# Attention scores in three terms, the low keys over 64 rows of the array

## The chip, the cores and the metric

The kernel runs on one core of one Trainium2 chip. The metric is the device time in microseconds. The engines are TensorE (PE, its weight loads PEld), VectorE (DVE), ScalarE (ACT), GpSimd (POOL) and the queue of SyncE (SP).

## The reference

Two layers over x of 2 x 1024 tokens of width 128. The part that the change touches is the attention of the first layer, 16 heads of width 64 over 1024 tokens of each of 2 batches:

```python
q = (x @ w_q).reshape(b, s, h, -1).transpose(0, 2, 1, 3)
k, v = jnp.split(x @ w_kv, 2, axis=-1)          # each to heads, as q
q = _l2norm(q) * jnp.exp(scale)
k = _l2norm(k)
sim = jnp.einsum('bhid,bhjd->bhij', q, k)
attn = jax.nn.softmax(sim, axis=-1)
out = jnp.einsum('bhij,bhjd->bhid', attn, v)
return out.transpose(0, 2, 1, 3).reshape(b, s, h * 64) @ w_out + b_out
```

After it come a residual and layer norm, a mixture of 8 experts (2 for each token), a norm, a state-space scan, a norm, a second mixture with a shared expert, and a norm. None of these is touched.

## The kernel before

The kernel holds numbers in two 16-bit parts, a high part (the number rounded to fp16, or cut to bf16 for the probabilities) and a low part (what is left), so that matmuls of fp16 come near to the precision of fp32.

The attention is cut into slots. A unit (h in the code, 16 of them) is two heads of one batch, and `bat` says which of its two heads. A slot is one head, 256 queries (QW) and 512 keys (KT = 4 key tiles of 128), so a head of a unit has 4 x 2 = 8 slots, a unit has SLOTS = 16, and there are 16 x 16 = 256 slots. The loop `heads` emits, on each engine, 32 slots (two units) for each i. In slot s:

- TensorE computes the scores (`scores`, L490) into the PSUM tile SC[s % 2], two banks of 512 columns, then the products of attention and values of the slot three before (`av`, L508; LAG = 3) into OP. In some slots it also transposes and multiplies the attention output of earlier units (L542, L550), projects tiles of the next unit (`proj`, L471 to L473) and transposes the next unit's queries and keys (`transposes`, L476, matmuls at L486). The slots of each of these are written out by hand in the tables GROUP_AT, TURN_AT, OUT_TURN_AT and OUT_AT.
- ScalarE takes the exponential of SC into Pr (L688), reads projections out of PSUM (L657, L658), makes the high part of the values (L665) and copies most of the transposes from the PSUM bank M1 into QK (L670).
- VectorE makes the low part Pl of the probabilities in 14 of 16 slots (L804), normalizes queries and keys (L777), casts their high parts into the stack `stk` (L786), copies the high keys a second time (L791) and reads OP (L823, L827).
- GpSimd makes Pl in the other two slots (L1033), inverse norms (L1040), low values (L1048) and the low parts of queries and keys (L1055).

The stack `stk` has, for each of 4 groups g of 4 token tiles, five cells of 64 columns (STK = 5 * DH): high queries, low queries, high keys, low keys, high keys again. `transposes` turns three pairs of neighbouring cells (128 columns each) into the three kinds of QK, each with 128 rows: kind 0 is high over low queries, kind 1 high over low keys, kind 2 low over high keys. A score is then two matmuls over 128 rows. Kind 1 times kind 0 gives high x high plus low x low, and kind 2 times kind 0 gives the two mixed terms:

```python
rhs = QK[:, b, 0, bat * S + q * QW:bat * S + q * QW + QW]
eng.matmul(out, QK[:, b, 1, key:key + P], rhs, start=True, stop=False)
mm = eng.matmul(out, QK[:, b, 2, key:key + P], rhs, start=False, stop=True)
```

The order around the change is kept by semaphores. Scores of slot n wait for the exponential of slot n - 2 (s_exps, L499), since SC has two buffers. The exponential waits for the scores and for a free Pr buffer (PB = 5, released by `av`). `av` waits for the low part of its slot (s_low_probs). The transposes wait for the high, copied and low parts of their group (s_qk_high, s_k_copied, s_qk_low). The first scores of a unit wait for the reads of all of its transposes.

Of the kernel before, what the change touches and what calls it, by code (L numbers as in the profile page):

```python
# [12 lines left out]
P = 128  # L13
B, S, D = 2, 1024, 128
T = B * S
NT = T // P
H, DH = 16, 64
# [8 lines left out]
def high(ap):  # L26

    return ap.bitcast(BF16)


def wait(eng, sem, count):

    if not isinstance(count, int) or count > 0:
        eng.wait_ge(sem, count)
# [12 lines left out]
QW = 256  # L47
KT = 4
# [6 lines left out]
TB = NT // B  # L55
# [28 lines left out]
def low_count(n, pool):  # L84

    mine = [k for k in range(SLOTS) if (k in POOL_LO) == pool]
    return n // SLOTS * len(mine) + sum(k <= n % SLOTS for k in mine)
# [44 lines left out]

CHUNK = 6
CHUNKS = 4


def chunk_tiles(c):

    return slice(CHUNK * c, min(CHUNK * c + CHUNK, TILES))


def sorted_rows(t):

    return t["w_or_rows"][:, 0:TILES * 2 * D].rearrange("p (j c) -> p j c", j=TILES)


def load_offsets(nc, t, ph, chunks=range(CHUNKS)):

    for c in chunks:
        _, values = nc.values_load_multi_w_load_instructions(  # L150
            t["at_w"][0:1, ph % 2, chunk_tiles(c)], engines=[mybir.EngineType.PE], min_val=0, max_val=(E - 1) * P,
            skip_runtime_bounds_check_because="the number of an expert was clamped to E - 1 before")
        for i, value in enumerate(values):
            t["weight_at"][ph, CHUNK * c + i] = value
# [96 lines left out]
def attention(nc, io, t):  # L251
# [3 lines left out]
    def sb(name, shape, dt):  # L255
        return es.enter_context(nc.sbuf_tensor(name, shape, dt))

    def ps(name, shape, dt):
        return es.enter_context(nc.psum_tensor(name, shape, dt))

    with es:
# [12 lines left out]
        nrm = sb("nrm", [P, 2, 4, 2, DH], F32)  # L274
        stk = sb("stk", [P, 4, 4, STK], F16)
        QK = sb("QK", [P, 2, 3, T], F16)
# [15 lines left out]
        SC = [ps(f"SC{i}", [P, KT, QW], F32) for i in range(2)]  # L292
# [29 lines left out]
        s_qk_high = sem("s_qk_high")  # L322
# [99 lines left out]
        def _(eng):  # L422
# [21 lines left out]
            rows = t["xs"][0].rearrange("(j p) c -> p j c", p=P)  # L444
            for c in range(CHUNKS):
                js = chunk_tiles(c)
                eng.dma_start(sorted_rows(t)[:, js, :], rows[:, js, :]).then_inc(s_rows_loaded, 16)
            eng.wait_ge(s_rows_loaded, 16 * CHUNKS)

        @block.tensor  # L450
        def _(eng):
# [24 lines left out]
            def transposes(h, j):  # L476
                g = j // 2

                wait(eng, s_qk_high, 4 * h + g + 1)
                wait(eng, s_k_copied, 4 * h + g + 1)  # L480
                wait(eng, s_qk_low, 4 * h + g + 1)
                m1 = M1[:, :].bitcast(F16)
                for kind in range(3):
                    at = (0, 2 * DH, 3 * DH)[kind]
                    for r in range(2):
                        mm = eng.transpose(m1[:, (2 * kind + r) * P:(2 * kind + r + 1) * P],  # L486
                                           stk[:, g, 2 * (j % 2) + r, at:at + P], ident16[:, :])
                mm.then_inc(s_turned, 1)

            def scores(i, s):  # L490
                n, h, b = 32 * i + s, 2 * i + s // SLOTS, s // SLOTS
                s %= SLOTS
                bat, q, kh = s // 8, s % 8 // 2, s % 2
                if s == 0:

                    wait(eng, s_turned_read_vector, 4)
                    wait(eng, s_turned_read_scalar, 8 * h + 4)

                wait(eng, s_exps, n - 1)  # L499
                for kt in range(KT):  # L500
                    key = bat * S + (kh * KT + kt) * P
                    rhs = QK[:, b, 0, bat * S + q * QW:bat * S + q * QW + QW]
                    out = SC[s % 2][:, kt, :]
                    eng.matmul(out, QK[:, b, 1, key:key + P], rhs, start=True, stop=False)  # L504
                    mm = eng.matmul(out, QK[:, b, 2, key:key + P], rhs, start=False, stop=True)  # L505
                mm.then_inc(s_scores, 1)

            def av(i, s):  # L508
                n, h, b = 32 * i + s, 2 * i + s // SLOTS, s // SLOTS
                s %= SLOTS  # L510
                bat, kh, u = s // 8, s % 2, s // 2

                pool = s in POOL_LO
                wait(eng, s_low_probs_pool if pool else s_low_probs, low_count(n, pool))
                if s == 0:

                    wait(eng, s_v_high, 4 * h + 4)
                    wait(eng, s_v_low, 4 * h + 4)
                if kh == 0:

                    wait(eng, s_outputs, 16 * i + 8 * b + u - 1)
                for kt in range(KT):
                    tile = bat * 8 + kh * KT + kt
                    for r in range(2):
                        hi = high(Pr[:, n % PB, kt, P * r:P * r + P])[:, 1::2]
                        lo = Pl[:, n % PB, kt, P * r:P * r + P]
                        at = (DH + 1) * r
                        first = kh == 0 and kt == 0 and r == 0
                        last = kh == 1 and kt == KT - 1 and r == 1
                        eng.matmul(OP[u % 2][:, at:at + 65], hi, V[:, b, tile, 0:65],  # L530
                                   start=first, stop=False, skip_group_check=True)
                        eng.matmul(OP[u % 2][:, at:at + 64], hi, V[:, b, tile, 65:129],  # L532
                                   start=False, stop=False, skip_group_check=True)
                        mm = eng.matmul(OP[u % 2][:, at:at + 65], lo, V[:, b, tile, 0:65],  # L534
                                        start=False, stop=last, skip_group_check=True)
                mm.then_inc(s_av_products, 1)
# [50 lines left out]
            def slot(i, s):  # L587
# [8 lines left out]
                if not ended(i):  # L596
                    scores(i, s)
                if s >= LAG and not ended(i):
                    av(i, s - LAG)
                elif s < LAG and started(i, 1):  # L600
                    av(i - 1, s + 2 * SLOTS - LAG)
# [34 lines left out]
            for j in range(PJ):  # L636
                m1_free(0, j, 0, 0)
                transposes(0, j)
# [120 lines left out]
        def _(eng):  # L759
# [20 lines left out]
            def high_parts(h, hb, g):  # L780
                G, b = 4 * h + g, g % 2
                wait(eng, s_normalized, G + 1)

                wait(eng, s_turned, 8 * (h - 1) + 2 * g + 2)
                out = stk[:, g, :, 0:4 * DH].rearrange("p t (k x) -> p t k x", k=2)[:, :, :, 0:DH]
                eng.tensor_copy(out, nrm[:, b, :, :, :]).then_inc(s_qk_high, 1)  # L786

            def copy_keys(h, hb, g):
                G, b = 4 * h + g, g % 2
# [237 lines left out]
        def _(eng):  # L1027
# [23 lines left out]
            def low_parts(h, hb, g):  # L1051
                G, b = 4 * h + g, g % 2
                wait(eng, s_qk_high, G + 1)
                both = stk[:, g, :, 0:4 * DH].rearrange("p t (k x) -> p t k x", k=2)
                eng.tensor_tensor(both[:, :, :, DH:2 * DH], nrm[:, b, :, :, :], both[:, :, :, 0:DH],  # L1055
                                  ALU.subtract).then_inc(s_qk_low, 1)

            def prepare(h, hb, s):
# [45 lines left out]
            for g in range(4):  # L1104
                if g < 3:
                    inverse_norms(0, 0, g + 1)
                low_values(0, 0, g)
                low_parts(0, 0, g)
# [82 lines left out]
def mixtures(nc, io, t, out):  # L1191
# [8 lines left out]
    with es:  # L1200
# [61 lines left out]
        s_gathered = [[sem(f"gathered{i}_{h}") for h in range(2)] for i in range(4)]  # L1262
        s_sorted_loaded = [sem(f"sorted_loaded{c}") for c in range(CHUNKS)]
        s_y_stored = [sem(f"y_stored{r}") for r in range(YR)]
# [18 lines left out]
        def _(eng):  # L1283
            def load(ph, c):
                J = TILES * ph
                js = chunk_tiles(c)

                eng.wait_ge(s_scattered[ph], 16 * 2 * TB)

                wait(eng, s_sorted_turned, J - TILES + js.stop)  # L1290
                rows = xs[ph % 2].rearrange("(j p) c -> p j c", p=P)
                eng.dma_start(xg[:, js, :], rows[:, js, :]).then_inc(s_sorted_loaded[c], 16)

            def store(ph, j):
                J = TILES * ph + j
                eng.wait_ge(s_down_read, J + 1)
                eng.dma_start(ys[ph % 2][P * j:P * j + P, :], yb[:, J % YR, :]).then_inc(s_y_stored[J % YR], 16)
# [22 lines left out]
            for j in range(TILES):  # L1320
                store(1, j)
            for c in range(CHUNKS):
                load(2, c)
            for j in range(TILES):
                store(2, j)
            for c in range(CHUNKS):
                load(3, c)
# [752 lines left out]
```

## Time and profile before

| | |
|---|---|
| time, median of 3 runs | 1051.43 us (1051.28 to 1055.02) |
| the profiled execution | 1044.7 us, its span 1042.9 us |
| mean granted TensorE clock | 0.944 of full |
| PE busy | 911.9 us, 87% |
| PEld busy | 856.1 us, 82% |
| ACT busy | 768.9 us, 74% |
| DVE busy | 732.2 us, 70% |
| POOL busy | 503.0 us, 48% |
| L504 and L505, scores | 1024 matmuls each, 273 ns each bar |
| L530, L532, L534, attention times values | 2048 matmuls each, 191 to 195 ns each bar |

A bar of a matmul is longer than the time until the next one starts, because matmuls are pipelined and their ends are modelled; the time that one costs TensorE is the distance between two starts. The span is divided in 40 slices of 26 us. The attention takes about the first 24 of them.

### The profile page before, as it was taken

The numbers are of one execution on the slowest core, as the hardware profiler recorded it, in microseconds if no ns is written. First come the engines' busy times: TensorE is split into PE (matmuls) and PEld (weight loads), VectorE is DVE, ScalarE is ACT, GpSimd is POOL, SyncE is SP. The second block draws the span as 40 slices with busy tenths as digits, with TensorE's granted clock in tenths as the row PEclk, the third lists the DMA queues.
The fourth block names the chain that finished last, engine by engine and source line by source line (L and its number), as shares of the span: only waits on it lengthen the run. The fifth ranks groups of instructions, "written<-read, shape, count | busy, mean of one in ns | idle before, by whom it ended". The sixth has DMA issues, their size and how long they took to land. (4 is left out here: it accounts for less than half of the span.)

```text
span 1042.9 us, 34710 instructions
## 1 busy us (share of the span) xinstructions
PE 911.9 (87%) x13676; PEld 856.1 (82%) x13676; DVE 732.2 (70%) x1432; ACT 768.9 (74%) x1275; POOL 503.0 (48%) x384
## 2 busy tenths in 40 slices
PE   4789999999999999999999997989969589899930
PEld 2678998998999989888889987989958479899830
DVE  6699989888988988888998974424549769400202
ACT  5689998998988999988889865445465366697831
POOL 5465655555554654644778800323327180052423
PEclk8799999999999999999999998999989689899965
DMA  8400000000000000000001020713111012023111
GB/s 256 130 2 3 23 3 23 2 3 22 3 3 22 3 3 23 3 3 23 9 8 37 13 63 7 231 55 91 45 29 31 1 36 64 16 72 98 57 57 43
DMA packets 43563, 42.13 MB, mean 40 GB/s; under 512 B 5648, under 2 KB 37392, under 8 KB 43408
## 3 DMA queue, kind: packets, MB, share of 16 engines
q1 hardware_dynamic: 39312, 31.51, 10.1%
q0 software_dynamic: 4096, 8.40, 2.6%
q8 instruction: 116, 1.90, 0.8%
q14 instruction: 39, 0.32, 0.1%
HBM read 25.60 MB, written 14.29 MB: 38 GB/s over the span
## 5 line engine op out<-in xcount | busy, mean ns | idle before, releaser
L688 ACT ACTIVATE Pr<-SC,nesc,esc 128x1024 f32<-128x1024 f32 x256 | 310.0, 1211 | 33.2 <-PE SC L505 22.9
L804 DVE TENSOR_TENSOR Pl<-Pr 128x1024 f16<-128x1024 f32 x224 | 293.2, 1326 | 39.7 <-ACT Pr L688 38.1
L504 PE MATMUL SC<-QK 128*128 128x256 f16 x1024 | 238.6, 273 | 1.0 <-ACT QK L670 1.0
L505 PE MATMUL SC<-QK 128*128 128x256 f16 x1024 | 238.6, 273 | 0.0
L530 PE MATMUL OP<-V,Pr 128*128 128x65 f16 x2048 | 214.4, 192 | 6.3 <-DVE Ob L827 6.2
L532 PE MATMUL OP<-V,Pr 128*128 128x64 f16 x2048 | 215.3, 195 | 0.0
L534 PE MATMUL OP<-V,Pl 128*128 128x65 f16 x2048 | 214.1, 191 | 0.0
L530 PEld LDWEIGHTS OP<-V,Pr 128*128 128x128 bf16 x2048 | 191.0, 97 | 13.4 <-issue 9.2
L532 PEld LDWEIGHTS OP<-V,Pr 128*128 128x128 bf16 x2048 | 190.0, 97 | 2.6
L534 PEld LDWEIGHTS OP<-V,Pl 128*128 128x128 f16 x2048 | 190.7, 99 | 0.0
L1055 POOL TENSOR_TENSOR stk<-nrm,stk 128x512 f16<-128x512 f32 x64 | 75.1, 1173 | 139.8 <-DVE stk L786 139.8
L1457 PE MATMUL DB<-wd,hid 128*128 (+1 forms) x864 | 124.9, 289 | 7.3 <-ACT hid L1589 3.2
L1960 POOL DMA_INDIRECT yg<-ys,slots x64 | 73.8, 1154 | 111.4 <-PE AB L1430 46.6
L670 ACT ACTIVATE QK<-M 128x768 f16<-128x768 f16 x124 | 101.0, 814 | 33.7 <-PE M L486 33.5
L1040 POOL TENSOR_TENSOR rn<-ss,half 128x8 f32<-128x8 f32 x64 | 108.5, 1696 | 17.7 <-DVE ss L767 11.2
L1457 PEld LDWEIGHTS DB<-wd,hid 128*128 128x128 f32 x864 | 107.5, 195 | 11.2 <-issue 8.4
L1033 POOL TENSOR_TENSOR Pl<-Pr 128x1024 f16<-128x1024 f32 x32 | 64.4, 2012 | 98.2 <-ACT Pr L688 98.1
L504 PEld LDWEIGHTS SC<-QK 128*128 128x128 f16 x1024 | 100.7, 98 | 10.5 <-issue 1.2
L505 PEld LDWEIGHTS SC<-QK 128*128 128x128 f16 x1024 | 100.4, 98 | 9.3
L1944 POOL DMA_INDIRECT xs<-split,slots x48 | 53.7, 1120 | 78.3 <-PE AB L1430 49.2
L1048 POOL TENSOR_TENSOR V<-raw,V 128x256 f16<-128x256 f32 x64 | 84.8, 1324 | 0.1
L486 PE MATMUL M<-ident,stk 128*128 128x128 f16 x768 | 66.2, 224 | 14.7 <-DVE QK L795 5.7
(224 smaller groups left out, 2168.2 us busy)
## 6 DMA issues: line engine op xcount, KB each, us to landing
ys<-yb SPq DMA_DIRECT2D x92, 64.0 KB, 1.5
w_or_rows<-xs SPq DMA_DIRECT2D x12, 384.0 KB, 4.2
wst<-in_up SPq DMA_DIRECT2D x8, 512.0 KB, 3.5
xs<-zero SPq DMA_DIRECT2D x2, 1472.0 KB, 13.4
scratch<-in_up SPq DMA_DIRECT2D x4, 576.0 KB, 4.5
wd<-in_wd SPq DMA_DIRECT2D x4, 576.0 KB, 5.8
wd<-in_wd SPq DMA_DIRECT2D x4, 512.0 KB
QK<-in_wqkv SPq DMA_DIRECT2D x4, 384.0 KB, 7.5
```

The source lines that it names most:

```text
L504: eng.matmul(out, QK[:, b, 1, key:key + P], rhs, start=True, stop=False)
L505: mm = eng.matmul(out, QK[:, b, 2, key:key + P], rhs, start=False, stop=True)
L530: eng.matmul(OP[u % 2][:, at:at + 65], hi, V[:, b, tile, 0:65], start=first, stop=False, skip_group_check=True)
L532: eng.matmul(OP[u % 2][:, at:at + 64], hi, V[:, b, tile, 65:129], start=False, stop=False, skip_group_check=True)
L534: mm = eng.matmul(OP[u % 2][:, at:at + 65], lo, V[:, b, tile, 0:65], start=False, stop=last, skip_group_check=True)
L670: eng.activation(QK[:, hb, :, 2 * P * j:2 * P * j + 2 * P], M1[:, :].bitcast(F16)[:, 0:6 * P].rearrange("p (k c) -> p k c", k=3), ACT.Copy ...
L688: eng.activation(Pr[:, n % PB, :, :], SC[s % 2][:, :, :], ACT.Exp, bias=nesc[:, hd:hd + 1], scale=esc[:, hd:hd + 1]).then_inc(s_exps, 1)
L804: eng.tensor_tensor(Pl[:, n % PB, :, :].rearrange("p a b -> p (a b)"), pr, high(pr)[:, 1::2], ALU.subtract).then_inc(s_low_probs, 1)
L1040: eng.tensor_tensor(rn[:, b, :, :], ss2[:, b, :, :], half[:, 0:1].unsqueeze(2).to_broadcast([P, 4, 2]), ALU.pow).then_inc(s_inverse_norms, 1)
L1048: eng.tensor_tensor(v[:, :, DH + 1:2 * DH + 1], raw[:, g, :, 2 * DH:QKV], v[:, :, 0:DH], ALU.subtract).then_inc(s_v_low, 1)
L1055: eng.tensor_tensor(both[:, :, :, DH:2 * DH], nrm[:, b, :, :, :], both[:, :, :, 0:DH], ALU.subtract).then_inc(s_qk_low, 1)
L1457: mm = eng.matmul(DB[:, 0:D], hid[:, u % HR, P * c:P * c + P], wd[l][c][:, at], start=c == 0, stop=c == NC - 1)
```

## The change

The low keys times low queries term is no longer computed. The other three are split otherwise: kind 1 of QK now holds the high keys twice, so that kind 1 times kind 0 over 128 rows gives high keys x (high + low queries). Kind 2 holds the low keys in one half of its rows and the high queries in the other: low keys above in even groups, below in odd groups. Low keys times high queries is a matmul over 64 rows. For that the five cells of `stk` are filled otherwise: low keys or low queries, high queries, low queries or low keys, high keys, high keys again. A slot's four key tiles are now two of an even group and two of an odd group (`key_tile`), so that two of them have their low keys in rows 0 to 63 and two in rows 64 to 127. They are issued alternately, and they write to different banks of SC. Only the first matmul into each bank carries `start`. `av` takes the value tiles in the same order. The number of matmuls and weight loads of each kind stays the same.

```diff
+def key_tile(kh, kt):
+    return 4 * (kt // 2) + 2 * kh + kt % 2
+
+def cells(stack, g):
+    return stack[:, g, :, :].rearrange("p t (c x) -> p t c x", c=5)
...
                 for kind in range(3):
-                    at = (0, 2 * DH, 3 * DH)[kind]
+                    at = ((1, 3, 0), (0, 3, 1))[g % 2][kind] * DH
...
                 wait(eng, s_exps, n - 1)
+                queries = slice(bat * S + q * QW, bat * S + q * QW + QW)
                 for kt in range(KT):
-                    key = bat * S + (kh * KT + kt) * P
-                    rhs = QK[:, b, 0, bat * S + q * QW:bat * S + q * QW + QW]
-                    out = SC[s % 2][:, kt, :]
-                    eng.matmul(out, QK[:, b, 1, key:key + P], rhs, start=True, stop=False)
-                    mm = eng.matmul(out, QK[:, b, 2, key:key + P], rhs, start=False, stop=True)
+                    key = bat * S + key_tile(kh, kt) * P
+                    eng.matmul(SC[s % 2][:, kt, :], QK[:, b, 1, key:key + P], QK[:, b, 0, queries], start=kt % 2 == 0,
+                               stop=False, skip_group_check=True)
+                for kt in (0, 2, 1, 3):
+                    key, half_of = bat * S + key_tile(kh, kt) * P, kt // 2
+                    part = slice(DH * half_of, DH * half_of + DH)
+                    mm = eng.matmul(SC[s % 2][:, kt, :], QK[part, b, 2, key:key + P],
+                                    QK[part, b, 0 if q // 2 == half_of else 2, queries], start=False, stop=kt % 2 == 1,
+                                    skip_group_check=True)
                 mm.then_inc(s_scores, 1)
...
-                    tile = bat * 8 + kh * KT + kt
+                    tile = bat * TB + key_tile(kh, kt)
...
-                out = stk[:, g, :, 0:4 * DH].rearrange("p t (k x) -> p t k x", k=2)[:, :, :, 0:DH]
-                eng.tensor_copy(out, nrm[:, b, :, :, :]).then_inc(s_qk_high, 1)
+                eng.tensor_copy(cells(stk, g)[:, :, 1:4:2, :], nrm[:, b, :, :, :]).then_inc(s_qk_high, 1)
...
-                both = stk[:, g, :, 0:4 * DH].rearrange("p t (k x) -> p t k x", k=2)
-                eng.tensor_tensor(both[:, :, :, DH:2 * DH], nrm[:, b, :, :, :], both[:, :, :, 0:DH],
+                stack = cells(stk, g)
+                low = stack[:, :, 0:3:2, :] if g % 2 else stack[:, :, 2::-2, :]
+                eng.tensor_tensor(low, nrm[:, b, :, :, :], stack[:, :, 1:4:2, :],
                                   ALU.subtract).then_inc(s_qk_low, 1)
```

## Rows read from the trace of the kernel before

**Rows 1.** The page: PE's busy time, and the 40 slices.

```profile
PE 911.9 (87%) x13676; PEld 856.1 (82%) x13676; DVE 732.2 (70%) x1432; ACT 768.9 (74%) x1275; POOL 503.0 (48%) x384
...
PE   4789999999999999999999997989969589899930
...
DVE  6699989888988988888998974424549769400202
ACT  5689998998988999988889865445465366697831
...
PEclk8799999999999999999999998999989689899965
```

**Rows 2.** Stretches: start:end, length, busy us of each engine, clock, DMA share, GB/s.

```profile
130.00:208.00 78.00, 76.56 (x1363) 72.34 (x1361) 69.21 (x124) 70.95 (x105) 44.21 (x33) 1.00 0.03 9
...
286.00:364.00 78.00, 76.55 (x1348) 72.30 (x1345) 68.30 (x119) 70.03 (x102) 42.99 (x29) 1.00 0.03 9
```

**Rows 3.** Groups from 130 to 600 us: busy us, mean ns | idle before.

```profile
L688 ACT ACTIVATE Pr<-SC,nesc,esc 128x1024 f32<-128x1024 f32 x203 | 245.7, 1210 | 23.1 <-PE SC L505 14.2
L804 DVE TENSOR_TENSOR Pl<-Pr 128x1024 f16<-128x1024 f32 x177 | 233.7, 1335 | 30.0 <-ACT Pr L688 28.5
...
L504 PE MATMUL SC<-QK 128*128 128x256 f16 x812 | 188.3, 273 | 0.0
...
L505 PEld LDWEIGHTS SC<-QK 128*128 128x128 f16 x811 | 79.3, 98 | 7.1
```

**Rows 4.** Waits from 130 to 600 us: total us, times, longest us.

```profile
DVE Pl L804 <- ACT Pr L688: 28.5, 30, 1.7
ACT QK L670 <- PE M L486: 19.6, 29, 2.2
...
PE M L550 <- issue: 5.2, 11, 1.1
...
PE OP L530 <- DVE Ob L827: 2.0, 7, 0.4
```

**Rows 5.** Timeline from 300 to 306 us, PE of one slot: start us, length us.

```profile
301.43 0.27 PE L504 MATMUL SC<-QK 128*128 128x256 f16 x1
...
301.54 0.27 PE L505 MATMUL SC<-QK 128*128 128x256 f16 x1
...
302.20 0.27 PE L505 MATMUL SC<-QK 128*128 128x256 f16 x1
...
302.31 0.19 PE L530 MATMUL OP<-V,Pr 128*128 128x65 f16 x1
...
302.34 0.20 PE L532 MATMUL OP<-V,Pr 128*128 128x64 f16 x1
...
303.04 0.25 PE L471 MATMUL M<-w_or_rows,xT_hi 128*128 128x192 f16 x1
...
303.54 0.50 PE L486 MATMUL M<-ident,stk 128*128 128x128 f16 x6
...
303.87 0.27 PE L504 MATMUL SC<-QK 128*128 128x256 f16 x1
```

**Rows 6.** Timelines of PE at 308 and at 310.6 us: the output's matmuls.

```profile
308.06 0.41 PE L542 MATMUL M<-ident,Ob 128*128 128x128 f32 x2
308.31 0.25 PE L471 MATMUL M<-w_or_rows,xT_hi 128*128 128x192 f16 x1
...
310.68 0.61 PE L550 MATMUL M<-wo,OT 128*128 128x128 f32 x4
```

**Rows 7.** Timeline of ACT: the first and the last exponential of 256.

```profile
36.98 1.21 ACT L688 ACTIVATE Pr<-SC,nesc,esc 128x1024 f32<-128x1024 f32 x1 [2.13 <-PE SC L505]
...
618.62 1.21 ACT L688 ACTIVATE Pr<-SC,nesc,esc 128x1024 f32<-128x1024 f32 x1 [0.41 <-PE SC L505]
```

**Rows 8.** Timeline of PE where the attention ends and the next part begins.

```profile
631.53 0.61 PE L550 MATMUL SC<-wo,OT 128*128 128x128 f32 x4
637.60 0.37 PE L1387 MATMUL XB<-ident,w_or_rows 128*128 128x128 f16 x2 [5.47 <-PEq L169]
```

## The prediction

> **What bounds the kernel now.** I read the page first, then the stretches of the attention part, then the single instructions of one slot. On the page [rows 1] TensorE is at 87% of the span; in the first 24 of the 40 slices it stands at 9 tenths nearly throughout while VectorE and ScalarE stand at 8 or 9 beside it, and from slice 25 on the last two are thin. The change touches only the attention part, so only that part is weighed. Its exponentials run from 36.98 us to 618.62 us [rows 7], 256 of them, so a slot (256 queries by 512 keys of one head) lasts 581.64 / 255 = 2.28 us. In the stretch from 130 to 600 us, 203 exponentials stand in 470 us [rows 3], 2.32 us for one, since the work of the first layer's routing is added there. I work by that stretch and scale by 256 slots.
>
> Three engines are close together there. By the stretches [rows 2] TensorE is busy 98% (76.56 of 78 us), ScalarE 90% (70.0 to 71.0), VectorE 88% (68.3 to 69.2), at full clock. Per slot of 2.32 us that is 2.08 us of ScalarE and 2.04 us of VectorE. TensorE's busy time says less, because a matmul's bar (0.27 us) is much longer than the step to the next one (0.11 us), so I add its need up from the starts [rows 5]:
> - scores: 8 matmuls of 256 columns, 301.43 to 302.31, 0.88 us (0.11 each);
> - attention times values: 24 matmuls of 64 or 65 columns, 302.31 to 303.04, 0.73 us (0.03 each);
> - projection of the next unit: 6 matmuls, 303.04 to 303.54, 0.50 us, in 8 of 16 slots;
> - transposes of the next unit: 6, 303.54 to 303.87, 0.33 us, in 8 of 16 slots;
> - output, in 4 of 16 slots: transposes 308.06 to 308.31, 0.25 us, and the product, four records about 0.11 apart, 0.44 us [rows 6].
> That is 1.61 + (8 x 0.83 + 4 x 0.69) / 16 = 1.61 + 0.59 = 2.20 us of the 2.32. TensorE stands still for about 0.12 us a slot. Little of it shows in the waits [rows 4] (2.0 us behind L827, 5.2 us at L550), since a wait shorter than the tail of the previous bar is covered by it. ScalarE and VectorE wait far more visibly: 19.6 us for the transposes, 28.5 us of VectorE for exponentials [rows 4], and those are the ordinary order of a ring in which TensorE is the slowest member. So TensorE bounds the attention part, by 0.12 to 0.16 us a slot over the next two. Behind the attention the last output product ends and the sorted rows begin to be used [rows 8]; nothing there overlaps with a slot, so time gained per slot arrives whole at the end.
>
> **The change part by part.**
> (a) Scores. Before, 4 key tiles x 2 matmuls over 128 rows. After, 4 matmuls over 128 rows (high keys doubled, times high and low queries) and 4 over 64 rows, in the order tile 0 (rows 0 to 63), 2 (rows 64 to 127), 1, 3. Low keys times low queries falls out. If the two row halves run side by side, the four take as long as two: 0.22 us instead of 0.44. Saving 0.22 us a slot, 256 x 0.22 = 56.3 us. No matmul in this trace uses less than all the rows of the array (every matmul row carries 128*128), so pairing is not shown. The bounds are 0 (the halves run one after the other, L504's step of 0.11 us each) and 0.22 us. I take 0.22, because the two halves share neither rows nor PSUM bank (tiles 0 and 1 lie in one bank, 2 and 3 in the other), and the number of weight loads stays at 8.
> The Trainium skill states the same of row halves ("TensorE: Matmul & The Clock Gate", Part 3: matmuls on distinct row groups start about 4 ns apart and run concurrently). By that page the saving would be those 0.22 us; no row here shows it.
> (b) Two changes of the array's division in each slot: from 128 rows to 64 before the halves, and back before L530. Such a step isn't in this trace. From below: 0, as between L505 and L530, where type, width and destination change and the step is still 0.11 us [rows 5]. From above: the whole tail of a matmul, 0.27 - 0.11 = 0.16 us, and on top the weight load of about 0.10 us that can no longer be done ahead 98 ns at L505 [rows 3]. I take what it takes to clear the rows of the array: 128 rows are passed in 128 steps, and 128 columns take 0.055 us here (0.33 us for six transposes of 128 columns); for 64 rows half of it, 0.03 us, the step of a 64-column matmul. An estimate from those two rows: 0.085 us a slot, 256 x 0.085 = 21.8 us. The bounds are 0 and 2 x 0.26 = 0.52 us a slot (133 us).
> (c) The stacks. L786 writes cells 1 and 3 instead of 0 and 2 (same 512 elements, same stride), L1055 writes cells 2 and 0 or 0 and 2 in blocks of 64 (same 512 elements), L791 is unchanged, the transposes begin at other cells. Counts, sizes and waits are the same. I take nothing; the backward block order at L1055 could cost at most some tenths of its 1.16 us per group on GpSimd, which is busy 44.0 of 78 us [rows 2] and is covered. The other order of key tiles only permutes columns, and L530 to L534 take the value tile to match.
> (d) What is late next. TensorE's need falls from 2.20 to 2.20 - 0.22 + 0.085 = 2.065 us. VectorE's 2.04 and ScalarE's 2.08 us are then level with it. With a lead of 0.12 to 0.16 us over the others the ring lost 0.12 us a slot; with no lead it should lose more, because any late low part (L804) or late read of M0 or M1 is passed on. I take 0.17 us instead of 0.12: + 0.05 x 256 = 12.8 us. Bounds: 0 (the loss stays) and 0.135 (the whole net saving of TensorE is given back and the slot is as long as before).
>
> Sum: - 56.3 + 21.8 + 12.8 = - 21.7 us. The profiled execution has a span of 1042.9 us and took 1044.7 us; it would come to 1023. The median of the runs is 1051.4, 6.7 us above it. None of the changed instructions has to do with that difference, so I keep it: 1051.4 - 21.7 = 1029.7, forecast 1030 us.
>
> **The rivals.**
> R1, the whole tail is paid at each change of division. The mechanism: the first matmul of the new division starts only when the last of the old one has left the engine entirely, 0.16 us after it could have started, twice a slot. TensorE's need becomes 2.20 - 0.22 + 0.32 = 2.30 us; + 0.10 x 256 = + 26 us, of which the ring may take back up to 0.05 a slot, as it would lose less: + 13 to + 26, so 1064 to 1077 us. It decides from the point at which the two changes together cost more than 0.22 us, 0.11 each. For it: the bars have that tail at every width (0.27 against 0.11 and 0.19 against 0.03 [rows 5]). Against it: the bars' ends are modelled, and the array itself has no cause to wait for a write into PSUM. With the weight load exposed as well (0.52 us a slot) it is + 0.30 x 256 = + 77 us, 1128 us.
> The Trainium skill speaks for this rival: "TensorEngine Tiling (Array Packing)", Key Properties, says that changing the tiling mode, as against the tile, drains the TensorE. It gives no duration, and no run here shows one yet.
> R2, the halves don't run side by side. Then (a) saves nothing, the switches stay: + 22 us less a little, about 1070 us. For it: no row shows a pair, and each half still needs its own weight load and its own 256 columns. Against: separate rows, separate banks.
> R3, the saving is eaten, by switches of about 0.10 us each or by the ring: VectorE and ScalarE at 2.04 and 2.08 us give the slot hardly less than today's 2.32 because their own waits (28.5 and 19.6 us, [rows 4]) stay. Within 5 us of 1051. For it: all three are above 88%. Against: those waits are for TensorE, and shrink as it gets faster.
> R4, the switches cost next to nothing. Then - 56.3 + 12.8 = - 43 us, 1008 us; TensorE's need would be 1.98 us, and VectorE and ScalarE would be the bound.
>
> **How the numbers follow.** Forecast case (gain of 10 to 32 us): 0.42. R4: 0.14. R3: 0.14. R1: 0.22, of which 0.06 with the load exposed. R2: 0.08. Differences below about 0.5% (5 us) can't be told from none here. Faster by more than that: 0.42 + 0.14 = 0.56, with a little of R3, 0.57. Same: 0.12. Slower: 0.22 + 0.08 + 0.01 = 0.31. The range reaches from R4 (1008) to the upper end of R1 without the load (1077); left out are the exposed load and a little on either side. The forecast's own range is 1019 to 1041.
>
> **What the next profile would show.** The starts of the four 64-row matmuls: two nearly together, the next two 0.11 us later (pairing), or all four 0.11 apart (R2). The step from the last 128-row score to the first half, and from the last half to L530: about 0.03 to 0.06 us above the normal 0.11 (forecast), 0.16 or more above (R1), none (R4). The slot, from exponential to exponential: 2.23 us in the stretch from 130 us on for the forecast, against 2.32. The busy share of VectorE and ScalarE should rise to over 90%, and TensorE's should fall. The prediction is wrong if a switch costs over 0.11 us, if the halves don't pair, or if ScalarE or VectorE turn out slower beside a faster TensorE.

## The result and the profile after

The changed kernel takes 1049.44 us, median of 20 runs, against 1052.16 us of the kernel before in 20 runs beside it. The ratio is 0.9972, with an interval of 0.996 to 0.9983: 3 us faster, within the 0.5% that was called no change. The forecast was 1030 us, a gain of 22 us; what came is the rival R3. The one profiled execution of the changed kernel happens to be longer than that of before (span 1048.8 against 1042.9 us). Its attention part isn't: the exponentials run from 36.40 to 617.34 us, 580.94 us against 581.64 us [rows 7]. Later experiments were run on more than one chip, whose times for the kernel before differ (1052.4, 1045.8 and 1054.2 us), so all comparisons between them go by ratios to the kernel before on the same chip.

The stretches of the changed kernel (start:end, length, busy us of PE, PEld, DVE, ACT, POOL, clock, DMA share, GB/s), beside [rows 2]:

```profile
130.00:208.00 78.00, 76.58 (x1355) 60.26 (x1352) 69.39 (x124) 70.85 (x104) 44.33 (x34) 1.00 0.03 9
...
286.00:364.00 78.00, 76.60 (x1358) 60.70 (x1355) 68.37 (x120) 70.25 (x102) 43.25 (x29) 1.00 0.03 9
```

In these two stretches TensorE, VectorE and ScalarE are as busy as before, to 0.2 us of 78. Only the weight loads changed: 60.3 instead of 72.3 us. One slot on PE, the same place as [rows 5] (start us, length us):

```profile
301.53 0.60 PE L513 MATMUL SC<-QK 128*128 128x256 f16 x4
302.06 0.39 PE L518 MATMUL SC<-QK 64*128 64x256 f16 x4
302.39 0.21 PE L545 MATMUL OP<-V,Pr 128*128 128x65 f16 x1
302.43 0.20 PE L547 MATMUL OP<-V,Pr 128*128 128x64 f16 x1
```

and in narrower windows, the last 128-row matmul and the first two over 64 rows, then the last two over 64 rows:

```profile
301.86 0.27 PE L513 MATMUL SC<-QK 128*128 128x256 f16 x1
302.06 0.28 PE L518 MATMUL SC<-QK 64*128 64x256 f16 x2
...
302.18 0.27 PE L518 MATMUL SC<-QK 64*128 64x256 f16 x2
```

The halves do run in pairs. Two matmuls stand in one bar of 0.28 us, where one alone has 0.27, and all four in 0.39, 0.11 more. The Trainium skill's page "TensorE: Matmul & The Clock Gate", Part 3, says this of distinct row groups, and the trace agrees: a pair starts within 0.01 us. But the step into the halves is 302.06 - 301.86 = 0.20 us and not 0.11. The last pair starts 0.12 after the first, at 302.18, and the first product with values comes 0.21 us later; a 256-column matmul alone asks for 0.11. The next step is 0.04 where [rows 5] have 0.03. From the first score to L545 it is 302.39 - 301.53 = 0.86 us, against 0.88 before: 0.22 saved, 0.20 paid again and 0.01 more on the step behind. The slot is no exception: in all 204 slots that start from 130 to 600 us the step into the halves is 0.20 to 0.21 us, and the step back is 0.20 at least.

The wait shows at the weight load too. Here is the load for the first product with values, before and after, with the load for the halves between them (start us, length us, idle time in front):

```profile
302.20 0.10 PEld L530 LDWEIGHTS OP<-V,Pr 128*128 128x128 bf16 x1
...
302.06 0.12 PEld L518 LDWEIGHTS SC<-QK 64*128 64x128 f16 x4 [0.21 <-issue]
302.38 0.10 PEld L545 LDWEIGHTS OP<-V,Pr 128*128 128x128 bf16 x1 [0.21 <-issue]
```

Before (first line), the load starts at 302.20 with the last score matmul, 0.11 us ahead of its own. After, the loads of the new division start together with their own matmul, at 302.06, or 0.01 ahead of it, at 302.38. The four loads of the halves stand in one bar of 0.12 us, which is why PEld is busy for less. The waits of PEld from 130 to 600 us (total us, times, longest us):

```profile
PEld SC L518 <- issue: 42.9, 204, 0.2
PEld OP L545 <- issue: 42.9, 192, 0.8
```

Once on each side of the halves, in nearly every slot of that stretch, the weight load stands for 42.9 / 204 = 0.21 us for nothing that another engine does.

### The profile page after: what moved, and what is told of

It is laid out like the page before. It is cut to its first block and busy times, and to the rows that moved or that the text cites. A ratio compares the mean times of both kernels' runs of the same rounds, so it can differ in the third digit from the quotient of the medians.

```text
span 1048.8 us, 34710 instructions
## 1 busy us (share of the span) xinstructions
PE 911.7 (87%) x13676; PEld 767.9 (73%) x13676; DVE 731.3 (70%) x1432; ACT 766.9 (73%) x1275; POOL 501.1 (48%) x384
## 5 line engine op out<-in xcount | busy, mean ns | idle before, releaser
L545 PEld LDWEIGHTS OP<-V,Pr 128*128 128x128 bf16 x2048 | 187.3, 97 | 60.4 <-issue 57.3
L545 PE MATMUL OP<-V,Pr 128*128 128x65 f16 x2048 | 217.7, 194 | 6.6 <-DVE Ob L841 6.6
L513 PE MATMUL SC<-QK 128*128 128x256 f16 x1024 | 155.0, 274 | 1.0 <-ACT QK L685 1.0
L518 PE MATMUL SC<-QK 64*128 64x256 f16 x1024 | 100.9, 276 | 0.0
L513 PEld LDWEIGHTS SC<-QK 128*128 128x128 f16 x1024 | 92.9, 98 | 8.1 <-issue 1.4
L1804 DVE TENSOR_TENSOR hid<-act,UB 128x512 f32<-128x512 f32 x46 | 31.6, 687 | 64.1 <-PE UB L1452 43.8
```

Source lines behind the costliest of these rows:

```text
L513: eng.matmul(SC[s % 2][:, kt, :], QK[:, b, 1, key:key + P], QK[:, b, 0, queries], start=kt % 2 == 0, stop=False, skip_group_check=True)
L518: mm = eng.matmul(SC[s % 2][:, kt, :], QK[part, b, 2, key:key + P], QK[part, b, 0 if q // 2 == half_of else 2, queries], start=False, stop ...
```

## The experiments

Two theories stood after this. Theory S: the saving was paid again by the two changes of the array's division, and TensorE sets the slot. Theory N: TensorE doesn't set the slot to the extent that I thought, so that even a free saving would not come through.

**Six matmuls over 128 rows, no change of division.**

```diff
-                    eng.matmul(out, QK[:, b, 1, key:key + P], rhs, start=True, stop=False)
-                    mm = eng.matmul(out, QK[:, b, 2, key:key + P], rhs, start=False, stop=True)
+                    mm = eng.matmul(out, QK[:, b, 1, key:key + P], rhs, start=True, stop=kt % 2 == 0)
+                    if kt % 2:
+                        mm = eng.matmul(out, QK[:, b, 2, key:key + P], rhs, start=False, stop=True)
```

> The kernel before with two of a slot's four second score matmuls (the mixed terms of key tiles 0 and 2) left out: six matmuls over 128 rows, 0.22 us less of TensorE a slot, and no change of the array's division. Theory S (the saving was paid out again by the two changes of division, the slot follows TensorE): the slot gets shorter by most of 0.22 us, 256 x 0.22 = 56 us at most, and I expect 35 to 50 us less than before, 1002 to 1017 us. Theory N (VectorE and ScalarE hold the slot, so that no saving on TensorE would come through): under 15 us less.

Measured: 1040.18 us against 1052.42, ratio 0.9886 (0.9859 to 0.9912), 12 us less. That is far under theory S's 35 and below theory N's bound of 15 us: of 56 us taken from TensorE about a fifth came through. The exponentials run from 35.82 to 605.58 us, 569.8 us. Where it stayed is seen in a slot in which the preparation of the next unit is under way. PE:

```profile
272.83 0.27 PE L506 MATMUL SC<-QK 128*128 128x256 f16 x1
273.94 0.19 PE L531 MATMUL OP<-V,Pr 128*128 128x65 f16 x1 [0.84 <-DVE Ob L828]
```

and DVE at the same time (x2 is two instructions in one row, from the start of the first to the end of the second):

```profile
268.26 2.35 DVE L805 TENSOR_TENSOR Pl<-Pr 128x1024 f16<-128x1024 f32 x2
270.53 1.14 DVE L778 TENSOR_TENSOR nrm<-raw,rn 128x512 f32<-128x512 f32 x1
271.71 0.43 DVE L787 CAST stk<-nrm 128x512 f16<-128x512 f32 x1
272.05 0.29 DVE L792 CAST stk<-nrm 128x256 f16<-128x256 f32 x1
272.25 0.68 DVE L764 TENSOR_REDUCE ss<-sq 128x8 f32<-128x512 f32 x1
272.96 0.43 DVE L768 TENSOR_SCALAR ss<-ss 128x8 f32<-128x8 f32 x1
273.31 0.16 DVE L824 RECIPROCAL rden<-OP 128x2 f32<-128x2 f32 x1
273.50 0.29 DVE L828 TENSOR_TENSOR Ob<-OP,rden 128x128 f32<-128x128 f32 x1
```

VectorE has no gap over 0.05 us in these 5.5 us. It reads OP (L828) at 273.50, and TensorE, whose last score started at 272.83 and which could have started L531 0.11 later, starts it at 273.94: 1.0 us lost, the saving of four to five slots. In the waits from 130 to 600 us that wait has grown from 2.0 us [rows 4] to 16.1 us:

```profile
PE OP L531 <- DVE Ob L828: 16.1, 23, 1.9
...
PE M L471 <- DVE x L837: 5.2, 11, 1.2
```

All waits of PE in that stretch grew from 13.0 to 41.4 us. The one for OP is half of the 28 us, and the second line, for VectorE too (1.7 us before), is another 3.5. Most of the rest, 11 us, stands before transposes and output matmuls and names no engine.

**The price alone.** The kernel before with the eighth score matmul over 64 rows:

```diff
-                    mm = eng.matmul(out, QK[:, b, 2, key:key + P], rhs, start=False, stop=True)
+                    part = slice(0, DH if kt == KT - 1 else P)
+                    mm = eng.matmul(out, QK[part, b, 2, key:key + P], rhs[part, :], start=False, stop=True)
```

> The kernel before with the last of a slot's eight score matmuls over rows 0 to 63 only (of the mixed terms of that tile, high keys times low queries is left out). Nothing is saved, eight matmuls of 256 columns remain, and the two changes of division are added. Theory S: the step in front of it 0.205 us instead of 0.11, the step behind it 0.20 us and about 0.01 on the first steps after each, 0.20 to 0.21 us a slot, so 35 to 52 us more than before, 1087 to 1104 us. Theory P (the long steps in the changed kernel come from the pairs, two matmuls and two weight loads at once, and not from the division): a single one costs little, within 15 us of before. Theory N: within 20 us, since the neighbours would hide it.

Measured: 1083.68 us against 1052.42, ratio 1.0297 (1.0274 to 1.032), 31 us more. Its PE timeline:

```profile
300.33 0.27 PE L506 MATMUL SC<-QK 128*128 128x256 f16 x1
300.44 0.27 PE L504 MATMUL SC<-QK 128*128 128x256 f16 x1
300.65 0.28 PE L506 MATMUL SC<-QK 64*128 64x256 f16 x1
300.86 0.20 PE L531 MATMUL OP<-V,Pr 128*128 128x65 f16 x1
```

Steps of 0.11, 0.21 and 0.21 us: a single half, not paired with anything, has the same long step on both sides. So it is the change of division and not the pair (theory P falls, its 15 us too). The two steps add 0.20 us a slot, 51 us in 256 slots, and 31 came out: a little under theory S's 35, and over theory N's 20. A part of the rest went into the waits that TensorE had anyway; from 130 to 600 us PE's waits are 3.0 us instead of 13.0. So a longer need of TensorE does lengthen the slot, while of a shorter one little came through.

**The halves in another order.** `for kt in (0, 1, 2, 3)` instead of `(0, 2, 1, 3)` for the 64-row matmuls:

> The changed kernel with the four 64-row matmuls in the order tile 0, 1, 2, 3: the two of rows 0 to 63 first, then the two of rows 64 to 127. Matmuls start in order. If only neighbours in different halves run at once, the starts are 0, 0.11, 0.114, 0.22: three steps of 0.11 instead of two, 0.11 us a slot more than the changed kernel. Theory S: 20 to 28 us slower than the changed kernel, 1070 to 1078 us. Theory N: no slower than the changed kernel by 10 us.

Measured: ratio 0.9983 (0.9968 to 0.9998), against 0.9972 of the changed kernel. Neither came: no 0.11 us was lost.

```profile
302.91 0.40 PE L518 MATMUL SC<-QK 64*128 64x256 f16 x4
303.24 0.20 PE L545 MATMUL OP<-V,Pr 128*128 128x65 f16 x1
```

All four still stand in 0.40 us, and L545 follows 0.33 us after the first, as before. The rows don't name the half of a matmul, so whether TensorE takes the free half's matmul first or otherwise keeps both busy stays open. As the trace itself didn't get longer, this run says nothing on theory N.

**The halves ahead of the 128-row matmuls.** Lines as in the changed kernel, the two loops exchanged, `start` on the first 64-row matmul of each bank:

> The changed kernel with the four 64-row matmuls ahead of a slot's four 128-row ones; all terms are computed. The change to 64 rows now follows matmuls of 64, 128 or 192 columns, the change back a matmul of 256. Theory F (a change costs a fixed time from the end of the last stream, 0.09 us, whatever its width, and 0.01 us on the next steps): the step from the last 65-column matmul to the first 64-row one is about 0.03 + 0.09 = 0.12 us, the step from the last 64-row one to the first 128-row one 0.20 us, and the time is within 4 us of the changed kernel. Theory W (what is waited for is the 256-column matmul and its results in PSUM): the first of these steps is clearly shorter, 0.03 to 0.06 us, and the kernel 15 us or more of TensorE better, of which some 4 to 8 us come through.

Measured: ratio 1.0 (0.9986 to 1.0015), 3 us above the changed kernel: within theory F's 4 us. PE:

```profile
300.98 0.25 PE L483 MATMUL M<-w_or_rows,xT_lo 128*128 128x192 f16 x1
301.15 0.39 PE L514 MATMUL SC<-QK 64*128 64x256 f16 x4
301.48 0.61 PE L519 MATMUL SC<-QK 128*128 128x256 f16 x4
...
303.16 0.50 PE L496 MATMUL M<-ident,stk 128*128 128x128 f16 x6
303.59 0.39 PE L514 MATMUL SC<-QK 64*128 64x256 f16 x4
```

and in one of the ten slots from 130 to 600 us in which the halves stand right behind the 65-column matmuls of attention times values:

```profile
258.76 0.19 PE L549 MATMUL OP<-V,Pl 128*128 128x65 f16 x1
258.88 0.28 PE L514 MATMUL SC<-QK 64*128 64x256 f16 x2
```

Behind a 192-column matmul, whose normal step is 0.08, the step into the halves is 0.17 us. Behind six transposes, normally 0.33 us [rows 5], it is 0.43. Behind 65 columns, normally 0.03, it is the 0.12 that theory F named. So what is added is 0.09 to 0.10 us behind 65, 128, 192 and 256 columns alike, a fixed time, and theory W falls. The way back follows the last half by 301.48 - 301.15 = 0.33 us from the first, as in the changed kernel. The attention lasts as long as there (36.67 to 617.78 us, 581.11 against 580.94), so that the 3 us of the ratio aren't found in it.

**Two slots' scores together,** to halve the number of changes: at the even slot its 128-row and 64-row matmuls, then the odd slot's 64-row and 128-row ones.

```diff
-                if not ended(i):
+                if not ended(i) and s % 2 == 0:
                     scores(i, s)
+                    scores(i, s + 1)
```

(Not shown: in `scores` the two loops also change places in odd slots, with `start` and `stop` to match.)

> The changed kernel with the scores of two slots computed one behind the other at the even slot, the even slot's 128-row matmuls first and the odd slot's 64-row matmuls first: one stretch of 64 rows for two slots, two changes of division instead of four. All terms are computed. Theory S: 0.10 us a slot less of TensorE than in the changed kernel, 15 to 26 us less if the two score buffers bear the earlier start of the odd slot, 1023 to 1034 us. If TensorE then waits for the exponential two slots back, this comes out as no gain or a loss, with waits of L518's successor for L703 in the profile. Theory N: no gain.

Measured: ratio 1.0028 (1.0014 to 1.0042), slower than the changed kernel by 6 us, but hardly by the wait that I named: the scores waited for exponentials 0.9 us in all, from 130 to 560 us, and their weight loads 6.2 us. What grew is

```profile
PE M L496 <- issue: 10.9, 23, 1.8
```

from 2.9 us in the changed kernel over the same stretch, before the transposes. The two scores come in a burst, and my reading is that the projections and transposes behind them run into reads by ScalarE and VectorE that are spaced by slots; no run tries that by itself.

**A lighter VectorE,** to see who holds TensorE's saving back. In `low_probs` of VectorE only (and one `memset`, before the loop, that puts 0 in the fourth tile's low parts):

```diff
-                pr = Pr[:, n % PB, :, :].rearrange("p a b -> p (a b)")
-                eng.tensor_tensor(Pl[:, n % PB, :, :].rearrange("p a b -> p (a b)"), pr, high(pr)[:, 1::2],
+                pr = Pr[:, n % PB, 0:KT - 1, :].rearrange("p a b -> p (a b)")
+                eng.tensor_tensor(Pl[:, n % PB, 0:KT - 1, :].rearrange("p a b -> p (a b)"), pr, high(pr)[:, 1::2],
```

> The kernel before, with VectorE making the low part of the probabilities for three of four key tiles only (768 instead of 1024 columns; the low part of the fourth tile is left out in those slots). VectorE has 0.28 us less in 14 of 16 slots, TensorE the same. Theory V (VectorE holds TensorE up in the slots where the preparation of the next unit lies, and takes savings of TensorE back): a little is gained, 10 to 25 us, since TensorE then only waits little and needs 2.19 us a slot. Theory A (ScalarE's reads of PSUM hold it up): under 8 us.

> The changed kernel with the same lighter VectorE (768 instead of 1024 columns of low parts). Its steps save TensorE only about 0.01 us a slot against the kernel before. Theory S (switches eat the saving): within 6 us of the same kernel before with the lighter VectorE, 1 to 6 us below it. If instead the changed score order was good and only VectorE hid it, it should be 20 us or more below.

> Six 128-row score matmuls (mixed terms of key tiles 0 and 2 left out) with the lighter VectorE (768 instead of 1024 columns of low parts). Theory V: the 0.22 us of TensorE now come through, 30 to 50 us below the kernel before with the lighter VectorE, about 990 to 1005 us. Theory A: VectorE's relief changes little, and it stays about 12 us below that kernel, near 1030 us.

Measured, as ratios to the kernel before: 0.9808 (0.9791 to 0.9824), 0.9804 (0.9787 to 0.982) and 0.9493 (0.9477 to 0.9509). The first is 20 us. In it TensorE is the bound: from 130 to 600 us its waits are 3.4 us in all, and the exponentials run from 37.45 to 601.13 us, 563.68 / 255 = 2.21 us a slot, about the 2.20 that the prediction had added up as TensorE's need. The second is the same, within the interval: where a shorter need of TensorE should show, the changed score order is worth at most 2 us (exponentials over 561.84 us), so it was not VectorE that hid its gain. Its own saving is gone, as theory S has it. The third is (0.9808 - 0.9493) x 1045.8 = 33 us below the first, against 12 us with the full VectorE. So VectorE held back more than a third of a true saving of 56 us (21 us), as theory V has it; theory A's 1030 us falls. In the light run with six matmuls (130 to 208 us) VectorE is busy 65.11 of 78 us, and no wait for L828 is left among those of PE (130 to 560 us):

```profile
130.00:208.00 78.00, 76.10 (x1412) 72.59 (x1409) 65.11 (x132) 74.39 (x114) 48.92 (x39) 1.00 0.03 9
...
PE M L486 <- issue: 5.6, 10, 1.5
PE M L543 <- issue: 5.1, 11, 0.5
PE M L551 <- issue: 2.8, 11, 0.8
```

ScalarE is at 74.39 of 78 there, 95%; it is the next in line, which may be why 23 of the 56 us still don't come. That last step is argued, not tried.

**GpSimd takes a third slot's low parts,** on the changed kernel: `POOL_LO = (1, 11, 15)` and `(1, 7, 15)`.

> The changed kernel with a third of the 16 slots' low parts (slot 11) made by GpSimd instead of VectorE; all terms are computed. VectorE has about 1.2 us less per unit just where the six-matmul run had its longest wait, GpSimd about 2 us more of its 57% busy time. Theory V: 2 to 8 us faster than the changed kernel, 1041 to 1047 us, as TensorE waits little with the switches in. If GpSimd is too late in slot 11 (its low part takes 1.95 us against 1.13), TensorE waits for it and the kernel gets slower.

> The changed kernel with the low parts of slot 7 (not 11) as the third of 16 made by GpSimd; all terms are computed. Slot 11's came too late, since GpSimd had low parts of keys of slot 10 in front of it. In slot 7 nothing else is queued on it. 2 to 6 us faster than the changed kernel if VectorE's relief arrives before slot 11; slower if the inverse norms of slot 8 come late behind it, which then holds L777's successor on VectorE.

Measured: 1.0051 (1.0034 to 1.0067) and 1.0115 (1.0094 to 1.0136), both slower than the changed kernel. With slot 11 TensorE waits for GpSimd's low part itself (6.2 us from 130 to 560 us), with slot 7 for VectorE's read of OP:

```profile
PE OP L545 <- POOL Pl L1047: 6.2, 5, 1.7
...
PE OP L545 <- DVE Ob L841: 11.9, 13, 1.2
```

The second row is of the run with slot 7; in the changed kernel it is 2.2 us. Relief in mean load, in these two places, costs more than it gives; that GpSimd's late answer is behind the second one too was not tried.

**Half the changes, scores finished on time.** The odd slot's 64-row matmuls move up behind the even slot's, its 128-row ones stay:

```diff
                 if not ended(i):
-                    scores(i, s)
+                    scores(i, s, "wide")
+                    if s % 2 == 0:
+                        scores(i, s, "narrow")
+                        scores(i, s + 1, "narrow")
```

(Not shown: `scores` takes the name of one of its two loops, and `start`, `stop` and the semaphore go to the first and the last loop of a slot.)

> The changed kernel with the odd slot's four 64-row matmuls moved up behind the even slot's, its 128-row ones left where they were, so that scores are finished at the same times as now: two changes of division for two slots instead of four. All terms are computed. TensorE needs 0.10 us a slot less, 27 us in all; by the run with six matmuls a fifth of such a saving came through (12 of 56 us), so 4 to 8 us less than the changed kernel, a ratio to before of 0.990 to 0.994. If TensorE has to wait for the exponential of two slots back in the even slots, it is slower, and a wait of the second group of 64-row matmuls for L703's successor shows.

> The same order with the lighter VectorE (768 of 1024 columns of low parts; the fourth tile's low part is left out in 14 of 16 slots). By the light runs two thirds of a TensorE saving come through there (33 of 56 us): 14 to 20 us below the light version of the changed kernel (ratio 0.980), so a ratio of 0.961 to 0.967. Were VectorE not what takes savings back, it would be 4 to 8 us as without it.

Measured: 0.9944 (0.9931 to 0.9958), and 0.9716 (0.9697 to 0.9734) with the lighter VectorE. The first is the fastest of those that compute all that the changed kernel does: 6 us below the kernel before, 3 below the changed one. Eight halves instead of four stand in one stretch here, and the odd slot (first two lines) has no long step:

```profile
301.81 0.60 PE L515 MATMUL SC<-QK 128*128 128x256 f16 x4
302.24 0.19 PE L551 MATMUL OP<-V,Pr 128*128 128x65 f16 x1
...
303.87 0.60 PE L515 MATMUL SC<-QK 128*128 128x256 f16 x4
304.41 0.61 PE L522 MATMUL SC<-QK 64*128 64x256 f16 x8
304.95 0.20 PE L551 MATMUL OP<-V,Pr 128*128 128x65 f16 x1
```

The scores of two slots take 0.43 + 1.08 = 1.51 us of TensorE, against 2 x 0.88 = 1.76 before: 0.12 us a slot less, 32 us in 256 slots.

Both gains are at the low edge of what I expected or below it: 3 us for 4 to 8, and (0.9804 - 0.9716) x 1054 = 9 us for 14 to 20. The expected wait for an exponential isn't there (0.3 us). In the waits from 130 to 560 us that for VectorE's read of OP has grown to 6.1 us, and in the light version 5.6 us stand before the transposes:

```profile
PE OP L551 <- DVE Ob L850: 6.1, 19, 0.7
...
PE M L496 <- issue: 5.6, 7, 1.7
```

## Why the prediction was wrong

(a) Right. The halves pair, and save 0.22 us a slot. The bound that I took from L504's step and the choice of the upper end hold. R2 falls.

(b) Wrong, and this is the step that decided. I took 0.055 us for the change to 64 rows and 0.03 for the change back, from the columns that fill 128 and 64 rows. Measured are 0.09 to 0.10 us each, the same in both directions, and about 0.01 on the step behind: 0.20 us a slot instead of 0.085, in 256 slots 51 us instead of 21.8. With it, and nothing given back in (d), as hardly a saving is left, the sum is - 56.3 + 51 = - 5 us, near the 3 us that came. My picture was wrong in kind and not only in size: by it the way back should have cost half as much as the way there, and it costs the same. The estimate also let the weight load go ahead as usual, and in the trace the load of the new division doesn't (it stands 0.21 us, twice a slot). The bounds of 0 and 0.26 each held, and the middle was too far down. How much of the 0.09 us is the old matmul leaving the array and how much is the load that is no longer done ahead isn't separated by any run. The Trainium skill's "TensorEngine Tiling (Array Packing)", Key Properties, says that a change of mode drains the TensorE. The trace agrees as far as that each change adds 0.09 to 0.10 us, which is less than the 0.16 us that R1 made of it; that this time is the drain is not shown.

(c) Right as far as can be seen: VectorE's and GpSimd's busy times changed by 0.3 us of 78 at most [rows 2], and the low parts, with the backward blocks, took 1160 ns against 1159.

(d) Not put to the test by the change itself, since TensorE's need fell by hardly 0.02 us. The runs show that it was far too small all the same. I gave back 0.05 us a slot of a net saving of 0.135. The run with the odd slot's halves moved up has nearly that saving, 0.12 us a slot, and 6 of its 32 us came: 0.10 a slot was taken back, though its matmuls also come in another order. With a saving of 0.22 us the ring took back 44 of 56 us, 0.17 a slot. I had compared means over the stretch, 2.20 us against 2.04 and 2.08, and so VectorE seemed to have room. In the slot shown above, with the preparation of the next unit, it has none and works through without a gap, and Pr and OP didn't carry the difference over to the slots where it idles. The lighter VectorE shows that this held back 21 of the 44 us; the other 23 stay open. With (b) right and (d) as it was, the sum would still have been too hopeful: with free changes of division the gain would have been about 12 us, as with six matmuls, and not the 43 of R4.

The rivals: R3 came, at a chance of 0.14, and by the first of its two mechanisms (0.10 us a change). Its counter-argument, that the neighbours' waits are for TensorE and shrink with it, is what the run with six matmuls refutes. R1's point of decision, 0.11 us a change, was well placed; the chip lies just below it. For the same reason the sign of being wrong that I named, a switch over 0.11 us, did not appear although the forecast failed: it parts slower from faster, and not a gain of 22 us from none. The chance of 0.57 for faster rested on (b) above all, for which no row stood in the trace.

## What to carry to other kernels

- Count the changes of the array's division, not only the columns saved. Here a pair of 64-row matmuls saved 0.11 us and a stretch of them cost 0.20, so with two pairs next to nothing is left and a stretch must hold more to gain; with four pairs in one stretch it was the fastest of the kernels that leave nothing more out.
- In a ring of three engines at about 90%, a mean need per slot doesn't say whose slack is real. Look at the slots in which the neighbour has no gap. One run that leaves the work out, with no other cost, prices the saving before it is built: here 12 us of 56.

## What the runs showed of the hardware that was not expected

- A change between 128 and 64 rows adds 0.09 to 0.10 us to the step: to 64 rows behind 65, 128, 192 or 256 columns, and back behind 256, for one half or for four. The weight load of the new division isn't done ahead of it.
- Four 64-row matmuls of 256 columns take the same 0.39 to 0.40 us, where four over 128 rows take 0.60, whether the program alternates the halves or lists one half's two first.
